# Cross-attention with experts on one core: a shared expert in high and low parts, and three reordered places

## What is computed

```python
q = decoder_feature @ Wq.T; k = encoder_feature @ Wk.T; v = encoder_feature @ Wv.T
lam = exp(sum(lambda_q1*lambda_k1)) - exp(sum(lambda_q2*lambda_k2)) + 0.8
att = softmax(q . k / sqrt(8));  att = att[:, :, 0] - lam * att[:, :, 1];  out = att @ v
# ffn
shared = silu(x @ ws_gate) * (x @ ws_up) @ ws_down
scores = sigmoid(x @ gate_w.T);  topk_w, topk_idx = top_k(scores, 2)
routed = sum over the two experts of topk_w * (silu(x @ w_gate[e]) * (x @ w_up[e])) @ w_down[e]
return routed + shared
# the whole
x = x + xattn(ctx, layernorm(x));  x = x + ffn(layernorm(x))
```

## Time and profile before

| | us |
|---|---|
| median of 3 runs | 2138.11 (2124.88 to 2149.83) |
| profiled execution | 2130.88 |
| its span | 2129.1 |
| granted TensorE clock in it, mean | 0.968 |
| busy PE | 1967.5 (92%) |
| busy DVE | 1616.4 (76%) |
| busy ACT | 1464.5 (69%) |
| busy POOL | 1441.6 (68%) |

### The profile page before, as it was taken

The page is one execution under the profiler, slowest core; times in us unless marked ns, Lnnn a source line. Parts: engine busy times, 40 slices in busy tenths (PEclk is TensorE's granted clock), DMA queues, the critical chain, the costliest instruction groups (busy, mean ns, idle before and its releaser), DMA issues.

```text
span 2129.1 us, 76257 instructions
## 1 busy us (share of the span) xinstructions
PE 1967.5 (92%) x20840; PEld 1418.7 (67%) x20840; DVE 1616.4 (76%) x4623; ACT 1464.5 (69%) x3511; POOL 1441.6 (68%) x2183
## 2 busy tenths in 40 slices
PE   3899999999999999999999999999989699999997
PEld 2555666666666666666666666666655599989996
DVE  2667788888778878888788887778776777767775
ACT  2567778777778777787787877777766455545554
POOL 4346677777677777677777777777656566656665
PEclk8799999999999999999999999999999799999999
DMA  4766676667666767666667676666774688868885
GB/s 122 195 189 194 186 199 189 203 203 199 190 185 196 204 189 196 194 195 194 198 194 201 190 200 193 192 190 191 212 211 161 206 266 263 259 200 274 256 267 172
DMA packets 606681, 432.00 MB, mean 203 GB/s; under 512 B 437572, under 2 KB 552395, under 8 KB 606161
## 3 DMA queue, kind: packets, MB, share of 16 engines
q1 hardware_dynamic: 546288, 319.87, 54.4%
q0 software_dynamic: 32256, 84.47, 10.9%
q10 hardware_dynamic: 28000, 26.03, 4.0%
HBM read 234.59 MB, written 197.72 MB: 203 GB/s over the span
## 4 chain that ended last, share of the span: by engine, by line
PE 54%; DMA 15%; SPq 14%; issue 7%; DVE 6%; POOL 3%; ACT 1%; DVEq 0%; POOLq 0%; ACTq 0%
DMA stacks<-mxT 8%; PE mx_ps L493 8%; SPq L369 7%; PE o_ps L526 6%; PE ms_ps L777 5%; PE ms_ps L554 5%; SPq L361 3%; SPq L354 3%; DMA stack_dram<-w_dn_sb 3%; PE mx_ps L554 3%; DMA stacks<-stack_dram 3%; PE mx_ps L556 3%; PE mx_ps L555 3%; PE ms_ps L555 3%; PE st_ps L755 3%
## 5 line engine op out<-in xcount | busy, mean ns | idle before, releaser
L981 DVE TENSOR_REDUCE mx<-mx_ps 128x4 f32<-128x512 f32 x1024 | 696.6, 686 | 234.4 <-PE mx_ps L493 229.7
L825 ACT ACTIVATE prob<-st_ps 128x512 f32<-128x512 f32 x1024 | 607.7, 596 | 318.4 <-PE st_ps L486 299.0
L493 PE MATMUL mx_ps<-stacks 48*128 48x128 bf16 x4096 | 397.7, 221 | 84.3 <-DMA stacks<-mxT 62.9
L486 PE MATMUL st_ps<-stacks 50*128 50x128 bf16 x4096 | 397.0, 221 | 0.0
L493 PEld LDWEIGHTS mx_ps<-stacks 48*128 48x128 bf16 x4096 | 232.4, 95 | 240.6 <-issue 130.5
L526 PE MATMUL o_ps<-prob,v_sb 128*32 128x256 f32 x4096 | 334.0, 398 | 0.9 <-ACT oT L812 0.6
L1343 POOL DMA_INDIRECT rows_dram<-rowt,posi x256 | 253.7, 991 | 67.9 <-issue 63.7
L554 PE MATMUL ms_ps<-e_lo 128*128 128x256 f32 x768 | 269.5, 351 | 18.6 <-DVE rowt L1080 9.8
L486 PEld LDWEIGHTS st_ps<-stacks 50*128 50x128 bf16 x4096 | 230.6, 95 | 2.6 <-issue 1.5
L555 PE MATMUL ms_ps<-e_lo 128*128 128x256 f32 x768 | 222.8, 290 | 0.0
L556 PE MATMUL ms_ps<-e_lo 128*128 128x256 f32 x768 | 221.8, 289 | 0.0
(11 more groups left out here) (155 smaller groups left out, 4667.3 us busy)
## 6 DMA issues: line engine op xcount, KB each, us to landing
stacks<-stack_dram SPq DMA_DIRECT2D x512, 192.0 KB
stack_dram<-w_dn_sb SPq DMA_DIRECT2D x192, 256.0 KB
stacks<-rows_dram SPq DMA_DIRECT2D x288, 130.0 KB
stack_dram<-w_dn_sb SPq DMA_DIRECT2D x64, 384.0 KB
stack_dram<-w_dn_sb SPq DMA_DIRECT2D x192, 128.0 KB
w_dn_sb<-in_x SPq DMA_DIRECT2D x64, 256.0 KB
w_dn_sb<-in_ctxT SPq DMA_DIRECT2D x64, 256.0 KB, 3.2
x_res<-in_x SPq DMA_DIRECT2D x64, 256.0 KB
```

Of the source, the lines that this page charges most:

```text
L486: return pe.matmul(st_ps[k % 2][:, i * P:(i + 1) * P], k_st[p][64 * h:64 * h + KROWS, u, j, :], q_st[p][64 * h:64 * h + KROWS, u, j, :], s ...
L493: return pe.matmul(mx_ps[k % 2][:, i * P:(i + 1) * P], q_st[p][64 * h:64 * h + ROWS, u, j, :], k_st[p][64 * h:64 * h + ROWS, u, j, :], sta ...
L825: nc.scalar.activation(prob[k % 4][:, :], st_ps[k % 2][:, :], ACT.Exp, scale=float(HALF) ** -0.5).then_inc(a_exp, 1)
L981: v.tensor_reduce(mx[:, u, c * CHUNK:(c + 1) * CHUNK], mx_ps[k % 2][:, :].rearrange("p (c n) -> p c n", c=CHUNK), AX.X, ALU.max).then_inc( ...
```

## The change

1. **Shared expert.** `gate_up` and `shared_down` become `product`s of high and low parts. ACT makes the high parts of the second norm's output (`a_hh`, slot 2) and of the hidden values (slot 9), POOL the low part of the first (`normed_low`, behind residual(d,2)), DVE the low part of the second (`shared_low`, slot 10). The shared weights are split once, early. The slots move: route 3 to 4, gate_up 3 and 5 to 5 and 6, shared_down 8 and 9 to 12, ranks 11 to 9; on DVE best_two 7 to 6, choice 8 to 7, shared_hidden 6 to 8, places 12 to 10, positions 13 to 11, shared_add 9 to 12. ACT's tanh moves from slot 5 to 7. In M0 shared_down now stands behind the ranks.
2. **SP's queue.** One `load_stacks` call (two transfers of 192 KB) moves from ahead of the Q put and `put_max` to behind them.
3. **Experts' loads.** Each 2 MB transfer becomes eight of 256 KB; `load_down` moves from step NS to NS-2. The last `expert_high` moves from (NS+1, 7) to (NS, 15), the last `expert_low` from behind the last `shared_add` to the start of DVE's last step.
4. **Start.** The four transfers of lambda get a semaphore of their own. The split of the weights moves into the first step (ACT slot 8, DVE slot 3), so the first norm stands ahead of it; PE waits for the weights only at its first project(0). POOL's two fills of `k_st` and its tables move into later steps. Some semaphores are merged.

The core of the diff:

```diff
@@ SP, step
+                if it.k is None and it.off == NS - 2:
+                    load_down()
                 if it.k is None and it.off in (NS - 1, NS):
                     load_experts(it.off - NS + 1)
-                    if it.off == NS:
-                        load_down()
                 if b.is_in(0, NS):
                     load_stacks(b, 1, 1)
-                    load_stacks(b, 1, 0)
                 if n2.is_in(0, NS):
                     put_parts(n2, 0, qp, d_qw, Q_RUNS[:1])
                 if it.is_in(0, NS):
                     put_max(it, 1)
+                if b.is_in(0, NS):
+                    load_stacks(b, 1, 0)
@@ PE
             def gate_up(k):
                 for h in range(DK):
-                    mm = pe.matmul(M1[:, k * SW:(k + 1) * SW], ws_gu_sb[:, h, k * HID:(k + 1) * HID], h2T[:, h, :],
-                                   start=(h == 0), stop=(h == DK - 1))
+                    mm = product(M1[:, k * SW:(k + 1) * SW], [w[:, h, k * HID:(k + 1) * HID] for w in (gu_hi, gu_lo)],
+                                 [x[:, h, :] for x in (h2_hi, h2_lo)], h == 0, h == DK - 1)
...
-                users = {"M0": (((a_v, 1, b, 1),), ((a_e, 1, r, 1),), ((v_base, 1, r, 1),), ((v_pf, 1, r, 1),),
+                users = {"M0": (((a_v, 1, b, 1),), ((a_e, 1, r, 1),), ((v_pf, 1, r, 1),), ((v_base, 1, r, 1),),
                                 ((a_k, 2, a, 2),)),
-                         "M1": (((v_x, 1, a, 1),), ((v_sh, 1, r, 1),), ((v_q, 1, a, 1),), ((a_h, 1, d, 1),)),
+                         "M1": (((v_x, 1, a, 1),), ((v_sh, 2, r, 1),), ((v_q, 1, a, 1),), ((a_h, 1, d, 1),)),
...
+                if k in (5, 6) and do_r:
+                    if k == 5:
+                        clear(it, "M1", 1)
+                        wait(pe, a_hh, 1, r, 1)
+                        wait(pe, g_hl, 1, r, 1)
+                    mm = gate_up(k - 5)
...
+                if k == 12 and do_r:
+                    clear(it, "M0", 3)
+                    wait(pe, a_sh, 2, r, 2)
+                    wait(pe, v_sh, 2, r, 2)
+                    for u in range(2):
+                        mm = shared_down(M0, u)
@@ ACT
+                    if k == 2 and do_r:
+                        wait(act, a_h, 1, r, 1)
+                        nc.scalar.activation(rnd(h2_hi[:, :, :]), h2T[:, :, :], ACT.Copy).then_inc(a_hh, 1)
+                    if k == 9 and do_r:
+                        wait(act, v_sh, 2, r, 1)
+                        nc.scalar.activation(rnd(sh_hi[:, :]), sh_h[:, :], ACT.Copy).then_inc(a_sh, 1)
@@ DVE
                     if k == 6 and do_r:
-                        shared_hidden(r)
+                        best_two(r)
                     if k == 7 and do_r:
-                        best_two(r)
+                        choice(r)
                     if k in COMBINE_AT and do_c:
                         combine(it, COMBINE_AT.index(k))
                     if k == 8 and do_r:
-                        choice(r)
+                        shared_hidden(r)
+                    if k == 10 and do_r:
+                        shared_low(r)
@@ POOL
+            def normed_low(s):
+                wait(gp, a_hh, 1, s, 1)
+                g.tensor_tensor(rnd(h2_lo[:, :, :]), h2T[:, :, :], h2_hi[:, :, :], ALU.subtract).then_inc(g_hl, 1)
...
                 if do_d:
                     residual(d, 2)
+                if do_r:
+                    normed_low(r)
```

236 lines of the change are left out of this document (135 added, 101 removed).

## The result

| | before | after |
|---|---|---|
| median of 3 runs, us | 2138.11 | 2321.04 (2319.96 to 2323.76) |
| span of the profiled execution, us | 2129.1 | 2322.0 |
| granted clock in it, mean | 0.968 | 0.909 |
| ratio after to before | | 1.086 (95% interval 1.076 to 1.096) |

The forecast was 2158, 0.9% up. The sign came true, the size did not: the time lies far above the range, which ended at 2205. Nor had "slower" (by more than 1%) been the likeliest outcome: it had 0.39, "same" 0.47.

A forecast was written before the change was run, and what follows sets the result against it. PE bounds the kernel, about 23.3 to 23.5 us of work in a 24.53 us step. Terms sum to +0.8, taken as +0.55 a step; times 60 +33, less 4.5 and 1.5, +27 on 2130.88: 2158 us, range 2100 to 2205.

The forecast's parts named there:

- slower: Whole kernel: outcome of a time more than 1% up, above 2159 us; chance 0.39.
- same: Whole kernel: outcome of a time within 1% of before, between 2117 and 2159 us; chance 0.47.
- SP's queue, -0.84: SP's queue: with two loads moved behind, PE's whole wait for `mxT` goes, -0.84 us a step, 0.4 as lower bound.
- Arithmetic, -0.3: Shared expert on PE: three products replace the float32 matmuls, -0.3 us a step, from 0.1 to 0.7.
- GpSimd, +0.55: gate_up at slot 5 on PE: new wait for POOL's `normed_low`, 0.55 us a step, from 0.4 to 0.9.
- ACT: ACT's list: three more copies, at 69% busy, new work ahead of waiting consumers by slots; no wait counted.
- DVE, +1.44: project(0) at slot 9 on PE: new wait for DVE's `shared_hidden`, 1.44 us in each step, bounds 1.2 and 1.7.
- the clock follows the wait: Rival, PE's clock after the new wait: two steps in three lose 1.7 us, +68, with half 2192 us; chance 0.14.
- Ends: Start and end of the phase: first K products some 4.5 us earlier, end -1.5 us, from -5 to +2.

The follow-up runs named there:

- shared_fp32: Kernel after with the shared expert in float32 again, slots and order of before on PE, ACT, DVE and POOL: 2115.01 us, ratio 0.988 to before.
- filled4: Kernel after with 20 matmuls whose result nothing reads ahead of project(0), filling PE's wait for `sh_h`; short setting: 2226.46 us, ratio 1.038 to before.
- early_low3: Kernel after with shared_hidden in slot 7, choice in slot 8 ahead of combine, route behind its slot's transposes, normed_low first in GpSimd's step: 2140.65 us, 0.999 of before.
- best: Kernel after with shared_hidden in slot 7, choice in 8 ahead of combine, route behind transposes, shared_down in 11, shared_add ahead of rest: 2206.87 us, 1.033 of before.
- after_ctl2: Kernel after, unchanged, measured again as a control in the long setting: 2455.11 us in a single execution, 1.067 of before.
- after_ctl: Kernel after, unchanged, measured again as a control in the short setting: 2317.59 us, ratio 1.084 to before.
- before_ctl: Kernel before, unchanged, measured again as a control in the short setting: 2138.34 us, 24.56 us a step.
- before_sp: Kernel before with only SP's queue changed, one load_stacks call behind the Q put and put_max; long setting: 2272.78 us, ratio 0.999.

## Why the forecast went wrong

Point by point, by its own steps.

- **SP's queue, -0.84.** Right that the wait goes: it is gone in the kernel after, and in shared_fp32 40.4 us became 9.6. Half of it went into other waits of 0.4 us, so the net was -0.49 with all that is not the first part.
- **Arithmetic, -0.3.** About right. PE's busy time of a step, taken to full clock, is 23.2 us before ((24.53 - 1.11 idle) x 0.99) and 22.7 to 23.0 in filled4 (without the filling) and early_low3: -0.2 to -0.5.
- **GpSimd, +0.55: measured 0.25.** The time of the result was right (7.97 us into the step in the kernel after, median, against 7.9 to 8.2). The arrival of PE was not: 7.86 instead of 7.3 to 7.5, 0.31 of it because `route`, ahead of gate_up, itself waits for `v_sb`. In best, where `route` doesn't wait and the low part comes 0.4 later, the wait is 1.12 in the step shown.
- **ACT.** I had given its list no wait; it is 0.31 for `v_sb`, small in this result. In the long setting it is 0.98, and it is the wait behind which the clock falls. A piece of work that is moved must be asked which bank it finds occupied.
- **DVE, +1.44: the first step that failed.** Mechanism and place were right, and with `hot` at 0.22 us, in the long setting, the wait is 1.35. But the sum left out `hot`. It had been behind the awaited instructions; it now stands ahead of them, in the very time when GpSimd runs `c_low`, and takes 1.29. In the step shown above slot 8's maxima start at 907.70 on PE, and by the forecast its reduction would have started 0.43 later, at 908.13; it started at 909.29. That is 1.16 late, 1.07 of it `hot`'s excess. `combine` and `shared_hidden` took 0.05 more than counted, and PE itself came 0.25 later: 1.44 + 1.16 + 0.05 - 0.25 = 2.40, the wait of that step; the mean is 2.31.
- **The clock: the second, and larger.** The forecast's sum has no loss by the clock at all, it even gives some back. I gave the rival "the clock follows the wait" 0.14, priced at half its full size, with the remark that it decides from a wait of about 1.5 us on. The wait was 2.31, in each step. The earlier trace rows had shown a stretch of that kind and its cost of 1.7 us; filled4 puts it at 1.96 a step. The remark itself does not hold as a rule of length: waits of 0.98 for `v_sb` were followed by the lower clock in 38 of 45 steps of after_ctl2, and waits of 1.35 for `sh_h` in 1 of 42.
- **Ends.** PE's first K product started at 20.55 us, and not after 25.69: 5.1 us earlier, where 4.5 was said. Over the whole no gain of the ends shows beyond some 7 us; shared_fp32 shows none.

The sum with the measured terms, a step: new waits (108.4 + 14.1 + 11.7) / 46.5 = +2.89, old ones gone -1.09, arithmetic -0.3, clock +1.96: +3.46, where +3.45 was measured. So close an agreement is luck, since the arithmetic alone is known only to within 0.3 and the clock's term comes from another kernel. The clock is more than half of it. The deeper fault was to treat the size of the wait and the fall of the clock as separate cases with separate chances, when the second depends on the first, and an error of 0.9 us in the first went with it. Whether a wait of 1.4 for `sh_h` would have left the clock up in the short setting was not measured.

## What to carry to other kernels

When an instruction is moved ahead of one that TensorE waits for, look at what GpSimd does at that moment, not only at its own length: a comparison of two SBUF operands went from 0.22 to 1.29 us. A wait of TensorE that recurs in every step can cost twice, once itself and once by the slow stretch behind it. Its length alone does not tell; look in the trace which wait the slow stretches follow, and test that one by filling it with matmuls that nothing needs. Here an arithmetic saving of some 0.3 us a step did not pay for the passes on other engines whose results it waits for, even with the order mended.

## What the runs showed of the hardware

- **The collision.** The same instruction takes 0.21 us when it starts 0.07 us after GpSimd's subtraction of 1.27 has ended, and 1.29 when it starts 0.07 after its start. Lengths between the two occur as well: it ends some 0.08 us behind the subtraction, wherever within it it starts (0.34 us when it starts 1.01 in, in one step of after_ctl; 0.22 to 1.03 in 31 steps of early_low3, 0.08 to 0.16 behind).
- **Behind which waits the clock falls.** In the kernel after behind the waits for `sh_h`, 2.31 us on average, in 46 of 47 steps, and in the step shown for 6 us at 0.51. In best behind 26 of the 50 waits of 1.17 for `h_lo` in slot 5, and behind none of the 51 waits of 1.03 for the places in slot 11; the mean clock was 0.96. In early_low3, with waits of 0.66 for `shared_add` in 53 steps, it was 1.00. In after_ctl2 behind 38 of 45 waits of 0.98 for `v_sb` in slot 4 and 1 of 42 waits of 1.35 for `sh_h`; the mean was 0.92. So waits of one length differ by their place in the step. That these waits are the cause and not only what precedes is shown by filling for `sh_h` in the short setting, and not for the others.
- **The two settings.** The kernel before takes 2138 to 2143 us in some runs and 2276 to 2300 in others; one chip gave 2300 at one time and 2143 at a later one. The matmul's mean (0.292 us) and those of ACT's instructions (0.48) and DVE's reductions (0.57) are the same in before_ctl and before_sp within 1%; what is longer is the idle time between them, as the wait for `v_sb` in the kernel after, 14.1 us in 46 steps against 44.3 in 45. About two thirds of it lie behind the attention phase: from PE's last maxima to the end it is 507 us in before_ctl and 591 in before_sp, which differs from it in SP's order only. A stretch of the second phase in the two:

```profile
1750.00:2050.00 300.00, 294.75 (x2164) 272.41 (x2164) 218.68 (x590) 162.19 (x589) 193.37 (x197) 0.99 0.82 253
1750.00:2050.00 300.00, 266.60 (x1813) 226.34 (x1811) 170.81 (x493) 127.40 (x492) 162.63 (x165) 0.98 0.70 213
```

The transfers move 213 GB/s instead of 253 and PE gets through 1813 matmuls instead of 2164, at nearly the same clock. The cause stays open. As most of the moves were measured in the long setting only, the share of the collision alone in the short one stays an inference, from `hot`'s length and from the wait of 1.35 where it doesn't collide.
